# Correlation of pass one with the stationary and the moving operand swapped: the inverse matrix held, the spectra streamed, the lags turned back

## What is computed

```python
qf = jnp.fft.fft(q, axis=2)
kf = jnp.fft.fft(k, axis=2)
corr = jnp.fft.ifft(qf * jnp.conj(kf), axis=2).real     # 64 lags for each channel
w, idx = jax.lax.top_k(corr.transpose(0, 1, 3, 2), 8)   # the 8 best lags of each channel
w = jax.nn.softmax(w, axis=-1)
# out[pos] = sum over i of w[i] * v[min(idx[i] + pos, 63)]
```

## Time and profile before

| | us |
|---|---|
| median of 3 runs (743.79 to 748.07) | 746.63 |
| the profiled execution, its own time | 746.08 |
| its span, first to last instruction | 744.2 |
| PE busy | 688.0 (92%) |
| DVE busy | 496.2 (67%) |
| ACT busy | 494.3 (66%) |
| POOL busy | 369.7 (50%) |

### The profile page before, as it was taken

One profiled execution on the slowest core, in us unless ns is written; L12 is line 12 of the kernel. 1 busy time (PEld: TensorE's weight loads), 2 busy tenths in 40 slices (PEclk: granted clock), 3 DMA queues, 4 the chain that ended last, 5 costly groups with the idle time before them and its releaser, 6 DMA issues.

```text
span 744.2 us, 12239 instructions
## 1 busy us (share of the span) xinstructions
PE 688.0 (92%) x3834; PEld 473.2 (64%) x3834; DVE 496.2 (67%) x1125; ACT 494.3 (66%) x881; POOL 369.7 (50%) x445
## 2 busy tenths in 40 slices
PE   8789999999987749799999999999999999999874
PEld 3344554545443437577877878878878878876663
DVE  3787878787742875676776776777677767756411
ACT  3567767675724978678688687697787786784110
POOL 1347777765534232443663563564554555554422
PEclk9999999999999979999999999999999999999997
DMA  7234444352212120101101101101101101000000
GB/s 242 87 99 129 114 141 123 110 174 77 85 57 103 43 79 22 43 1 58 42 16 57 42 14 56 42 14 56 42 14 56 42 14 56 14 15 29 0 15 29
DMA packets 25781, 45.69 MB, mean 61 GB/s; under 512 B 3184, under 2 KB 4976, under 8 KB 25744
## 3 DMA queue, kind: packets, MB, share of 16 engines
q1 hardware_dynamic: 25744, 45.24, 19.0%
HBM read 36.84 MB, written 8.39 MB: 61 GB/s over the span
## 4 chain that ended last, share of the span: by engine, by line
PE 85%; DVE 5%; ACT 5%; issue 3%; POOL 1%; POOLq 0%; DVEq 0%; ACTq 0%
PE ps_b L991 9%; PE ps_b L992 8%; PE ps_b L993 8%; PE wide L1088 7%; PE wide L991 4%; PE ps_b L1029 4%; PE wide L993 4%; PE wide L992 4%; PE bank L1059 4%; PE ps_a L1029 4%; PE wide L1049 4%; PE ps_b L1172 4%; PE ps_a L991 2%; PE ps_a L993 2%; PE ps_a L992 2%
## 5 line engine op out<-in xcount | busy, mean ns | idle before, releaser
L608 POOL TENSOR_TENSOR va<-mv,small 128x1 f32<-128x1 f32 x80 | 15.3, 191 | 141.4 <-DVE mv L971 81.8
L420 ACT ACTIVATE q_stack<-qt_h 32x512 fp32r<-32x512 f32 x128 | 80.6, 630 | 1.9
L688 POOL TENSOR_TENSOR y_l<-y,y_h 128x512 fp32r<-128x512 f32 x16 | 20.6, 1290 | 97.5 <-ACT y_h L550 97.5
L1088 PE MATMUL wide<-w_m,x1t 128*128 128x512 f32 x128 | 60.8, 619 | 0.7 <-ACT x1t L441 0.7
L991 PE MATMUL ps_b<-down_h,ht_h 128*128 128x512 f32 x128 | 53.9, 421 | 6.2 <-DVE ht_l L893 3.4
L900 DVE RECIPROCAL y<-ps_b 128x256 f32<-128x256 f32 x32 | 55.9, 1748 | 0.0
L991 PE MATMUL wide<-up_h,t_h 128*128 128x512 f32 x128 | 52.3, 408 | 1.2 <-DVE t_l L880 1.2
L677 POOL TENSOR_TENSOR kbd_b<-kt_h,small 128x512 bf16<-128x512 f32 x32 | 34.1, 1086 | 35.7 <-ACT kt_h L519 35.7
L993 PE MATMUL ps_b<-down_h,ht_l 128*128 128x512 f32 x128 | 51.2, 400 | 0.0
L992 PE MATMUL ps_b<-down_l,ht_h 128*128 128x512 f32 x128 | 50.9, 398 | 0.0
L993 PE MATMUL wide<-up_h,t_l 128*128 128x512 f32 x128 | 50.6, 396 | 0.0
(11 more groups left out here) (193 smaller groups left out, 2075.9 us busy)
## 6 DMA issues: line engine op xcount, KB each, us to landing
x_in<-in_x SPq DMA_DIRECT2D x16, 256.0 KB, 2.7
ctx_t<-in_ctx SPq DMA_DIRECT2D x16, 256.0 KB, 2.6
x_res<-in_x SPq DMA_DIRECT2D x16, 256.0 KB, 2.6
x_in<-x_rows SPq DMA_DIRECT2D x16, 256.0 KB, 2.7
ctx_t<-in_ctx_turned SPq DMA_DIRECT2D x16, 256.0 KB, 2.9
x_res<-x_rows SPq DMA_DIRECT2D x16, 256.0 KB, 3.6
out<-stage SPq DMA_DIRECT2D x16, 256.0 KB, 2.0
x_rows<-x SPq DMA_DIRECT2D x8, 256.0 KB, 2.4
```

The source lines that it names most:

```text
L420: last = act.activation(out[STACK * part:STACK * (part + 1), p, :], halves[STACK * p:STACK * (p + 1), :].bitcast(F32), ACT.Copy)
L1088: last = pe.matmul(bank[7], cols(x1t, c, P), cols(w0_m, c, D), start=(c == 0), stop=(c == DC - 1))
```

## The change

The product D is done the other way round: `icorr` is stationary and the spectra of one batch, 512 channels wide, move. Two matmuls instead of eight. Their result has the lags on the partitions (64 for each batch) and the channels along the row, so it has to be turned: ACT copies `bank[4]` into a new tile `lags`, and PE turns it by four transposes back into `bank[4]`, where DVE finds it as before. ACT's copy stands between L459 and L466 of its body, PE's transposes stand between F and G (called F' in the prediction), and DVE's `max` waits for the new semaphore `lag_ps` instead of `corr_ps`.

```diff
+        lags = one("lags", [P, D])
...
@@ ACT, body(i), behind the weight piece, ahead of the copy wt
+                t = i + 2
+                if live(t):
+                    act.wait_ge(S["corr_ps"], t + 1)
+                    act.activation(lags[:], bank[4], ACT.Copy).then_inc(S["lag_s"], 1)
...
@@ DVE, body(i)
                     corr = bank[4].rearrange("p (c s) -> p c s", s=SEQ)
-                    dve.wait_ge(S["corr_ps"], t + 1)
+                    dve.wait_ge(S["lag_ps"], t + 1)
                     for c in range(2 * DC):
                         top = dve.max(m8[:, c, :], corr[:, c, :])
...
@@ PE, body(i), step D
                     pe.wait_ge(S["prod_s"], t + 1)
                     wait(pe, S["shift_s"], t)
-                    for c in range(DC):
-                        for b in range(2):
-                            k = slice(P * c + SEQ * b, P * c + SEQ * (b + 1))
-                            last = pe.matmul(bank[4][:, k], prod[:, b, P * c:P * (c + 1)], icorr, start=True, stop=True)
+                    for b in range(2):
+                        last = pe.matmul(bank[4][SEQ * b:SEQ * (b + 1), :], icorr, prod[:, b, :], start=True, stop=True)
                     last.then_inc(S["corr_ps"], 1)
...
@@ PE, body(i), behind step F
                     transform(ps_b, V0, ctx_t).then_inc(S["v_ps"], 1)
+                    pe.wait_ge(S["lag_s"], t + 1)
+                    for c in range(DC):
+                        last = pe.transpose(cols(bank[4], c, P), cols(lags, c, P), ident)
+                    last.then_inc(S["lag_ps"], 1)
```

More of the change, by code:

```diff
@@ L236, in build @@
             nm1_s nb1_s nm2_s nb2_s x_loaded ctx_loaded res_loaded bn1_s mv1_s va1_s rs1_s xn1_s
-            q_ps qf_s k_ps prod_s v_ps vf_s vsw_s corr_ps tops_s shift_s exp_s rep_s sum_s inv_s sub_s wgt_s
+            q_ps qf_s k_ps prod_s v_ps vf_s vsw_s corr_ps lag_s lag_ps tops_s shift_s exp_s rep_s sum_s inv_s sub_s wgt_s
             wt_ps wt_s wf_ps prod2_s o_ps x1_s bn2_s mv2_s va2_s rs2_s xn2_s
```

## The result

The changed kernel takes 752.35 us (median of 6, 751.92 to 752.72) against 745.8 for the kernel before (6 runs, 743.72 to 749.04); the ratio is 1.0073 with a 95% interval of 1.0045 to 1.0100. The forecast was 747.9, no change that can be told, with a range of 743.5 to 751.5. So the time came out 4.5 us above the forecast, 0.9 above the upper end that the range names; the case "slower" had been given 0.15. (The upper ends of the terms behind that range, +2.7 and +3.2, add up to 752.5; the range stopped at 751.5.) Of the forecast, the closed path from D by way of `max`, exp and prod back to D was right as the thing that binds. Its length was not: 12.07 us a tile was expected, 12.73 came in most bodies.

The account below looks back on a forecast made before the run. The closed cycle from D through max, exp and prod, 12.07 us a tile, was taken to bind, not PE's 11.78. Twelve periods (-0.9) and both ends (+2.2) add 1.3 to 746.63: 747.9 us, range 743.5 to 751.5.

Parts of the forecast that it names:

- ACT's copy: ACT's copy of D's result out of PSUM: 0.60 us a tile, in idle time before wt, costing nothing.
- the case "slower": Whole kernel: slower by more than the 0.5% (3.7 us) that can be told; chance 0.15.
- the terms behind that range: Steady periods -2.9 to +2.7 us, both ends of pass one +1.2 to +3.2 us, plus 0.6% spread of runs.
- the closed path from D by way of `max`, exp and prod back to D: Pass one's steady bodies: this cycle sets the period, 12.07 us a tile against 12.145 before.
- PE's 0.37 us: PE's work per tile: D saves 0.91 us, F' adds 0.54, leaving 11.78 us; 0.29 of 0.37 becomes waiting.
- rival "PE stays the bound": Pass one: period is PE's 11.78 us, total 744.4 us, or 742.2 with the ends free; chance 0.13.
- From D to `max`: First link of the cycle: D 0.93, E 0.54, F 0.96, F' 0.54, release 0.11, together 3.08 us.
- second rival: PE's array changes form 7 times a body, not 5: cycle 12.37 us, +4.9, total 751.5; chance 0.14 with dearer D start.
- From exp to prod: Link from exp's start on ACT to prod's end on DVE: 6.90 us, unchanged while ACT never waits inside.
- From `max` to exp: Link from DVE's max to the end of its small subtraction: 2.00 us, plus some 0.04 to wake ACT.
- The ends: Pass one's first bodies +1.2 and an estimated +0.4 us, last tile +0.6: together +2.2 us.
- Sum: Whole kernel: -0.9 us from twelve steady periods and +2.2 from both ends of pass one, +1.3 us.

Follow-up runs that it names:

- the run with the turn ahead: The changed kernel with F' (PE's transposes of the lags) moved ahead of F (transform of the values): 741.15 us, ratio to the kernel before 0.9905.
- the run with narrow additions: The changed kernel with POOL's two additions to x2 done on one column instead of 512: 748.61 us in one execution, period 12.18 to 12.20 us.

## Why the prediction was right in kind and wrong in size

- **What bounds.** That PE's 0.37 us would not be gained, since the path through `max`, exp and prod closes just behind it, was right: PE waits ahead of D, DVE waits for the turn, ACT's exp waits for DVE. The forecast's rival "PE stays the bound" fell. But there weren't 0.37 us to gain. PE's steps without their waits add up to 12.0 us and not 11.78: E 0.59, F and G 1.06 each, F' 0.58, H 3.54, I 0.53, and for those that wait here, by the run with the turn ahead, A and B 0.96 each, C 1.77, D 0.96. The forecast took over E, F and G at their old lengths.
- **ACT's copy.** 0.597 us in idle time ahead of wt, as said; neither E nor G waits for it.
- **From D to `max`: 3.08 expected, 3.35 measured.** The price of the form changes (second rival) was sized too low, though it isn't the whole. F takes 1.06 with another form ahead of it and behind it and 0.96 with one only ahead; G takes 0.96 with one only behind, ahead of H, and 1.06 with both (the fence above and the run with the turn ahead). C takes 1.86 with both and 1.77 with one. E and F' have both now and take 0.59 and 0.58, where E had taken 0.54 with one. In the 0.27 that makes 0.10 for F, 0.05 for E and 0.04 for F'; the rest is D, 0.96 and not 0.93 when it doesn't wait, and 1.01 when it starts on a waiting array. The rival's total, 751.5, lies near the measured one by luck: its period was 12.37, and its signs (E over 1.05 us after D, F' over 0.65) didn't come.
- **From exp to prod: 6.90 expected, 6.75 measured.** I took ACT's run for gapless. It held a wait: qf started 0.64 us after x1t before the change and 0.48 after it (110.01 to 110.49); before, it waited for PE's A (its records, from 118.34 on, end at 119.47). When PE is no longer the bound, such a wait goes. With these two the cycle is 12.07 + 0.27 - 0.15 = 12.19, the period of the run with narrow additions. The rows of before, then of the changed kernel:

```profile
118.88 0.59 ACT L441 ACTIVATE x1t<-bank 128x512 f32<-128x512 f32 x1
...
119.52 1.02 ACT L446 ACTIVATE qf<-ps_a 128x1024 f32<-128x1024 f32 x1
```

```profile
110.01 0.59 ACT L442 ACTIVATE x1t<-bank 128x512 f32<-128x512 f32 x1
110.49 1.03 ACT L447 ACTIVATE qf<-ps_a 128x1024 f32<-128x1024 f32 x1
```

- **From `max` to exp: 2.00 expected, 2.55 measured.** This is the step that failed. I moved DVE's two subtractions by about 0.5 us against POOL and kept their length. Before, L826 ran from 114.35 to 114.59, and POOL's addition to x2 started at 114.47, 0.12 us behind it. The trace of before held a sign of what happens when POOL is first, at the last tile (lower two rows) and in the answer for that line (shortest, median, longest in ns):

```profile
114.47 1.28 POOL L655 TENSOR_TENSOR x<-x,x 128x512 f32<-128x512 f32 x1
...
198.24 1.27 POOL L655 TENSOR_TENSOR x_odd<-x_odd,x 128x512 f32<-128x512 f32 x1
...
198.84 0.75 DVE L826 TENSOR_TENSOR weight<-m 128x64 f32<-128x64 f32 x1
```

```profile
L826 DVE TENSOR_TENSOR weight<-m x16: 215/242/748, 16.3 to 198.8; 128x64 f32<-128x64 f32 x16
```

One of 16 took three times the median: the last tile's, which started while POOL's addition was running. The forecast used the median and didn't ask about the longest. The collision is worth 151.21 - 146.23 = 5.0 us over the twelve periods (the second number is that of the run with narrow additions), about the whole difference between forecast and result.
- **The ends.** +1.2 and an estimated +0.4 to the fourth D: 1.66 measured. That it fits so well is in part luck: the run with narrow additions has the same instructions up to there, since the first addition to x2 comes behind the fourth D, and took 37.22 us, +0.14; and the granted clock between these D was 0.86 before and 0.91 in the changed kernel. Behind the last D the forecast had +0.6. E of the last tile came 1.4 later, and by the last group of one of PE's steps in pass two (L1179 at 690.39; the same step before is L1172, at 682.61) the loss counted from the last D was 1.8. Only +0.3 is left at the end of the span because the last 60 us went faster, at a granted clock of 0.96 against 0.92.
- **Sum.** -0.9 + 2.2 had been forecast for span and median. Steady bodies 5.5, first bodies 1.7, the end 0.3, less 1.15 by which the first D came earlier: 6.3.

## What to carry to other kernels

When a change moves an engine's steps by a fraction of a us, look not only at who waits for them but at what runs beside them then: here a POOL operation started 0.12 us behind a DVE operation on SBUF, a margin that a shift of 0.5 us took away. A step that goes to another engine and back (copy, turn) may be worth more right behind that engine's work, even at a wait (PE waited 0.2 us for the copy), than where the engine has room, if a closed path runs through it; here the move was worth 12.73 - 11.98 = 0.75 us a tile, of which 0.54 is the collision that it avoids. The operands' swap alone was worth 0.36. And a chain read as gapless may hold waits for the very engine that is to become faster; take its length from the run after the change, or look for two of its links whose distance isn't their length.

## What was not expected of the hardware

- A DVE tensor_tensor of 128x64 with both inputs in SBUF takes 0.21 to 0.24 us alone and up to 1.32 when it starts 0.03 us behind a POOL tensor_tensor of 1.27 us; it ends about 0.08 us behind POOL's end in each case. The other way round the loss is small: POOL's addition took 1.34 when it started 0.01 us behind DVE, and 1.28 when it started 0.12 behind. A DVE subtraction of 128x512 with one input in PSUM isn't held (0.68 to 0.69).
- A step of PE with another form of the stationary tile on both sides takes about 0.1 us longer than with a change on one side (1.06 against 0.96; 1.86 against 1.77), four transposes 0.05 longer (0.59 against 0.54), at a granted clock of 1.00.
